# Decoder layer (state-space scan, pairwise sigmoid, mixture of experts): the stage in front of the scan reordered, the context sums taken off TensorE, high parts first, routing parts made after the second expert

## What is computed

```python
# block 1: Mamba2-like scan, 32 heads of 8, state 64, chunks of 128
xBC, z, A = split(LN(x) @ W_in.T)          # 256+2048+2048, 256, 32 columns
xBC = causal_conv4(xBC) + b; dt = softplus(A)
x = x + ((ssd_chunk_scan(...) + D * xc) * silu(z + z_bias)) @ W_out.T
# block 2: ctx is 4 x 256 x 64
si = ctx @ Wi; sj = ctx @ Wj
x = x + 0.6 * sigmoid(si[:, :, None] + sj[:, None, :] + b) + 0.4 * LN(x)
# block 3: 7 routed experts (top 2) and one shared, all of 256 x 256
u = xt @ Wup + bup; g = silu(u @ Wgate + bgate) * u
x = x + sum_e prob[e] * (g @ Wdown + bdown) + shared
```

## Time and profile before

| | |
|---|---|
| three runs | 432.19, 433.98 (median), 435.38 us |
| profiled execution, own time | 433.75 us |
| its span, first to last instruction | 432.0 us |
| mean granted TensorE clock | 0.976 |
| PE, PEld busy | 403.1, 304.4 us |
| DVE, ACT, POOL busy | 335.0, 227.7, 170.8 us |

### The profile page before, as it was taken

How to read it: one execution, slowest core, us unless ns; L and a number is a source line. 1 busy time by engine, 2 the same in 40 slices (tenths; PEclk the granted TensorE clock), 3 DMA queues, 4 the chain that set the end, 5 groups by cost and what they waited for, 6 DMA issues and landing times.

```text
span 432.0 us, 8785 instructions
## 1 busy us (share of the span) xinstructions
PE 403.1 (93%) x2989; PEld 304.4 (70%) x2989; DVE 335.0 (78%) x569; ACT 227.7 (53%) x411; POOL 170.8 (40%) x199
## 2 busy tenths in 40 slices
PE   3898999999999999999999996899999999939996
PEld 2686676676676676676666674568798888829896
DVE  4787689889898898898898838639966967826575
ACT  6766645455555455458776622474554544543631
POOL 3794110111110111105556820235675686564561
PEclk9999899999999999999999997799999999969999
DMA  7202201221012221115231140000202102000002
GB/s 213 61 1 55 57 10 56 59 59 55 15 49 56 59 57 38 29 54 132 66 100 23 47 149 2 0 0 2 74 2 73 51 24 74 0 1 2 0 1 99
DMA packets 34316, 20.54 MB, mean 48 GB/s; under 512 B 16072, under 2 KB 32144, under 8 KB 34288
## 3 DMA queue, kind: packets, MB, share of 16 engines
q1 hardware_dynamic: 34288, 20.18, 16.3%
HBM read 17.55 MB, written 1.31 MB: 44 GB/s over the span
## 4 chain that ended last, share of the span: by engine, by line
PE 79%; DVE 12%; ACT 3%; POOL 2%; issue 1%; DMA 1%; SPq 0%; DVEq 0%; ACTq 0%; POOLq 0%
PE bank L1186 28%; PE bank L1210 22%; PE bank L1413 8%; PE bank L1337 5%; PE bank L1401 4%; PE bank L1346 4%; DVE conv L963 3%; PE bank L1421 2%; PE bank L1196 2%; PE bank L1360 1%; POOL el L617 1%; DMA w_raw<-in_L_attn_W_in_dram 1%; DVE conv L1165 1%; PE bank L1381 1%; DVE utl L946 1%
## 5 line engine op out<-in xcount | busy, mean ns | idle before, releaser
L963 DVE SCALAR_TENSOR_TENSOR conv<-bank,taps,conv 128x510 f32<-128x510 f32 (+2 forms) x204 | 150.7, 745 | 25.9 <-ACT conv L650 21.1
L1210 PE MATMUL bank<-uth,parts 128*128 128x512 f32 x272 | 98.7, 413 | 2.9 <-DVE utl L946 1.6
L650 ACT ACTIVATE conv<-bank,tap_b,taps 128x512 f32<-128x512 f32 x68 | 52.9, 778 | 69.8 <-PE bank L1210 69.4
L527 POOL TENSOR_TENSOR ce<-conv,ecx 128x512 f32<-128x512 f32 x15 | 19.5, 1297 | 134.1 <-DVE conv L963 132.9
L612 POOL TENSOR_TENSOR ul<-conv,uh 128x512 fp32r<-128x512 f32 x32 | 42.7, 1349 | 48.7 <-ACT uh L865 31.0
L1210 PEld LDWEIGHTS bank<-uth,parts 128*128 128x128 f32 x272 | 51.6, 190 | 12.3 <-issue 2.2
L617 POOL TENSOR_TENSOR el<-conv,parts 128x512 fp32r<-128x512 f32 x30 | 44.0, 1489 | 34.8 <-ACT parts L877 34.7
L1210 PE MATMUL bank<-utl,parts 128*128 128x512 f32 x136 | 56.8, 418 | 0.0
L1153 DVE CAST uh<-conv 128x512 fp32r<-128x512 f32 x28 | 25.6, 949 | 28.4 <-ACT conv L861 28.1
L1048 DVE SCALAR_TENSOR_TENSOR g<-dec,bank 128x512 f32<-128x512 f32 x64 | 40.9, 679 | 1.8 <-PE bank L1337 1.7
L1413 PEld LDWEIGHTS bank<-conv 64*128 64x128 f32 x512 | 31.1, 187 | 13.9 <-DVE conv L963 7.4
(11 more groups left out here) (206 smaller groups left out, 763.2 us busy)
## 6 DMA issues: line engine op xcount, KB each, us to landing
w_raw<-in_L_attn_W_in_dram SPq DMA_DIRECT2D x17, 256.0 KB, 3.2
ecx<-ecum_dram SPq DMA_DIRECT2D x32, 128.0 KB, 2.9
ew_raw<-in_L_ffn_Wup_dram SPq DMA_DIRECT2D x7, 256.0 KB, 2.8
ew_raw<-in_L_ffn_Wgate_dram SPq DMA_DIRECT2D x7, 256.0 KB, 3.0
ew_raw<-in_L_ffn_Wdown_dram SPq DMA_DIRECT2D x7, 256.0 KB, 4.2
xres<-in_x_dram SPq DMA_DIRECT2D x2, 512.0 KB, 3.9
out_dram<-xres SPq DMA_DIRECT2D x4, 256.0 KB, 2.2
yi<-yev SPq DMA_DIRECT2D x56, 16.0 KB, 1.9
```

Of the source, the lines that this page charges most:

```text
L650: act.activation(conv[q][:, j, HALF * h:HALF * (h + 1)], bank[u % 2][:], ACT.Identity, bias=tap_b[q][:, j:j + 1], scale=taps[q][:, j, TAPS ...
L963: dve.scalar_tensor_tensor(out=dst[:, :, d:SEQ], in0=src[:, :, 0:SEQ - d], scalar=taps[q][:, j, TAPS - 1 - d:TAPS - d], in1=dst[:, :, d:SE ...
L1210: ins = pe.matmul(bank[u % 2][:], w, x_t, start=(i == 0), stop=(i == 3 * KD - 1))
```

## The change

Six parts:

1. Context sums: `si` and `sj` are now products on GpSimd (`weigh_context`, pair 1, two of 128x512) and reductions on VectorE (`sum_context`, end of pair 1). SP stores `sj` to DRAM in pair 3 and in pair 4 loads it back to every partition, one load for each sequence. TensorE's context transposes and matmuls and ScalarE's copies are gone; `halve_si` runs in pair 13.
2. The bf16 parts of the decays are made by GpSimd instead of VectorE; the table load for Exp moves from in front of the scan to the first `gate_of_z` (pair 12).
3. The order in front of the scan: project(0,0,2), (0,0,3), (1,1,0) each come one step earlier between the z tiles; W_out's transposes go to bank 7 at the end.
4. `up` and `gate` take the four matmuls of high token parts first, then the two of low parts, each with its own wait in front.
5. Between scan and experts: 9 and 3 `keep_warm` matmuls around the transposes of half 0; no `means_by_roots` where only the root is used; `shift` made later; the root for half 1 earlier on ScalarE; VectorE normalises all four tiles of half 1; gate(0) of half 0 after the transposes of half 1.
6. `prob3` is made by GpSimd after `el` of expert 1 instead of at the start of expert 6.

```diff
@@ SP
+                if n == 3:
+                    sp.wait_ge(sums_done, 2)
+                        sp.dma_start(sj_dram.rearrange("(t p) -> p t", p=P), sj[:]).then_inc(sj_out, 16)
+                if n == 4:
+                    sp.wait_ge(sj_out, 16)
+                    for b in range(NSEQ):
+                        sp.dma_start(sig[:, 2 * b, :], sj_dram[SEQ * b:SEQ * (b + 1)].partition_broadcast(P)).then_inc(sig_in, 16)
@@ GpSimd
+            pool.wait_ge(cum_done, 1)
+            link_parts(pool.tensor_copy(cparts[:, 0, :], cum[:]))
+            link_parts(pool.tensor_tensor(crest[:], cum[:], cparts[:, 0, :], ALU.subtract))
...
+            pool.tensor_copy(cparts[:, 2, :], crest[:]).then_inc(cpart_done, 1)
...
+            def weigh_context():
+                pool.wait_ge(ctx_sm_in, 32)
...
+                for i in range(2):
+                    pool.tensor_tensor(ctx_w[i], c_v, wij[:, :, CTX * i:CTX * (i + 1)].to_broadcast([P, T, CTX]),
+                                       ALU.mult).then_inc(ctx_weighed, 1)
...
+                        if isinstance(n, int) and n == 1:
+                            weigh_context()
...
-                if isinstance(e, int) and e == NE - 2:
...
+                if isinstance(e, int) and e == 1:
                     pool.wait_ge(prob_done, 1)
                     pool.tensor_copy(prob3[:, :, 2 * 32:2 * 32 + NE], prob[:])
@@ ScalarE
             def gate_of_z(v):
+                if v == 0:
+                    act.preload_act_table(ACT.Exp)
...
             normalise(T, range(2), 3)
             split_turned(4, 4)
+            split_turned(5, 5)
             root(slice(4, 8), 4)
-            split_turned(5, 5)
...
+                    if first and v == 1:
+                        root(slice(T + 4, 2 * T), 5)
                     if first and v == 2:
                         copy_logits(0)
-                        root(slice(T + 4, 2 * T), 5)
-                        normalise(T + 4, range(4, 6), 5)
@@ VectorE
-            link(dve.tensor_copy(cparts[:, 0, :], cum[:]))
...
+            def sum_context():
+                dve.wait_ge(ctx_weighed, 2)
+                for dst, v in ((si, ctx_w[0]), (sj, ctx_w[1])):
+                    dve.tensor_reduce(dst[:], v, AX.X, ALU.add).then_inc(sums_done, 1)
...
                         rest_w(n + 2, q)
+                    if u == 3 and isinstance(n, int) and n == 1:
+                        sum_context()
...
-            inverse_roots(slice(0, 4), 2, lambda: gate_last(1))
+            inverse_roots(slice(0, 4), 2, lambda: gate_last(1), False)
...
-            normalise(T + 6, range(6, 8))
+            normalise(T + 4, range(4, 8))
@@ TensorE, in front of the scan
             project_a()
             project(0, 0, 1)
             project_z(0)
+            project(0, 0, 2)
             project_z(1)
-            project(0, 0, 2)
+            project(0, 0, 3)
             project_z(2)
-            project(0, 0, 3)
+            project(1, 1, 0)
             project_z(3)
             pe.wait_ge(z_read, 2)
             turn_x(0)
             turn_x(1)
-            project(1, 1, 0)
...
+            project(1, 1, 1)
...
-            for i in range(2):
-                pe.matmul(bank[2 + i][:], wj_rep[:], ctxT[:, HALF * i:HALF * (i + 1)], start=True, stop=True).then_inc(pair_done, 1)
...
+            project(1, 1, 2)
+            turn_w(2, 1, 0, lambda: pe.wait_ge(misc_read, 1))
+            project(1, 1, 3)
             pe.wait_ge(wo_in, 16)
+            pe.wait_ge(cexp_done, 1)
@@ TensorE, after the scan
+            up_weights = ewh[0][:, 0, :, :].rearrange("p k d -> p (k d)")
+            pe.wait_ge(ewl_done, 3)
+            pe.wait_ge(o_read, 1)
+            keep_warm(2, up_weights, 9)
             turn_tokens(4, 4)
             turn_tokens(5, 5)
+            keep_warm(2, up_weights, 3)
...
+            def high_first(dst, highs, lows, before):
+                for i, (left, right) in enumerate(highs):
+                    before(i)
+                    pe.matmul(dst, left, right, start=(i == 0), stop=False)
+                for i, (left, right) in enumerate(lows):
+                    before(len(highs) + i)
+                    ins = pe.matmul(dst, left, right, start=False, stop=(i == len(lows) - 1))
...
@@ gate
-                    if m == 0:
-                        pe.wait_ge(ul_done, 4 * e + 2 * n + 2)
+                    def before(i):
+                        if m == 0 and i in (0, 2):
+                            pe.wait_ge(uh_done, 4 * e + 2 * n + i // 2 + 1)
+                        elif m == 0 and i >= 4:
+                            pe.wait_ge(ul_done, 4 * e + 2 * n + i - 3)
@@ expert 0
                     up(0, 0, range(2))
                     logits(0)
-                    gate(0, 0, range(1))
                     turn_tokens(6, 6)
                     turn_tokens(7, 7)
-                    gate(0, 0, range(1, 2))
+                    gate(0, 0, range(2))
```

More of the change, by code:

```diff
@@ L177, in decoder_layer @@
         ctx_raw = ew_raw[1][:, 0, :].rearrange("p (t d) -> p t d", t=T)
-        ctxT = ew_raw[1][0:CTX, 1:3, :].rearrange("p a n -> p (a n)")
+        ctx_w = [xn[:, 2 * i:2 * i + 2, :].rearrange("p t d -> p (t d)").rearrange("p (t d) -> p t d", t=T) for i in range(2)]
         def f32(ap):
@@ L491, in _, with copy_x @@
             pool.wait_ge(const_done, 3)
[L493 removed]
+            parts_made = [0]
+            def copy_x(m, q):
                 c0 = 2 * HD * (m - 1)
@@ L739, in pairwise @@
             def pairwise(u):
-                act.wait_ge(pair_read, 3)
+                if u == 0:
+                    halve_si()
+                    act.wait_ge(si_done, 1)
+                    act.wait_ge(sig_in, 16 * NSEQ)
                 for t in ((1, 3), (5, 7), (0, 2), (4, 6))[u]:
@@ L1086, in _ @@
             inverse_roots(slice(T, T + 4), 3)
+            shifts(range(4))
             normalise(T + 2, range(2, 4))
@@ L1299, in _ @@
             ins.then_inc(misc_turned, 1)
-            project(1, 1, 1)
             turn_x(2)
@@ L1310, in _ @@
                     c = (2 * k + j) * P
[L1311 removed]
+                    ins = pe.transpose(bank[7][:, c:c + P], wo_raw[:, j, k * P:(k + 1) * P], ident[:])
             ins.then_inc(misc_turned, 1)
[L1313 to L1325 removed]
+            pe.wait_ge(z_read, 4)
             def weigh(n, q, u):
@@ L1503, in up @@
                     at_least(pe, silu2_done, 4 * (e - 1) + v + 1)
-                    if isinstance(e, int) and e == 0 and m == 0:
-                        pe.wait_ge(utl_done, 6 + 2 * n)
-                    three(up_bank(e, v)[:], lambda k: [(ewh[q][:, 0, k, c], uth[:, k, s]), (ewh[q][:, 0, k, c], utl[:, k, s]),
-                                                 (ewl[q][:, 0, k, c], uth[:, k, s])], KD).then_inc(up_done, 1)
+                    def before(i):
+                        if isinstance(e, int) and e == 0 and m == 0:
+                            if i in (0, 2):
+                                pe.wait_ge(uth_done, 5 + 2 * n + i // 2)
+                            elif i >= 4:
+                                pe.wait_ge(utl_done, 5 + 2 * n + i - 4)
+                    high_first(up_bank(e, v)[:], [(w[q][:, 0, k, c], uth[:, k, s]) for k in range(KD) for w in (ewh, ewl)],
+                               [(ewh[q][:, 0, k, c], utl[:, k, s]) for k in range(KD)], before).then_inc(up_done, 1)
             def gate(e, q, tiles=range(4)):
```

133 lines of the change are left out of this document (58 added, 75 removed).

## The result

The changed kernel takes 420.9 us (median of four runs, 419.86 to 421.52) beside 434.13 for the kernel before: a ratio of 0.970, 95% interval 0.966 to 0.974, so 13.2 us less. The forecast was 420.0, with a range of 415.5 to 424.0. The profiled execution took 421.52, its span 419.8.

What follows compares the result with a forecast made beforehand. Bounds: TensorE waits in expert 6 and after the scan, a chain before it, TensorE's pace in the scan, the GpSimd-ScalarE-VectorE circle in experts. From 433.75, -6.5 +0.9 +0.4 +0.3 -8.6 = -13.5 gives 420.25, stated 420.0; range 415.5 to 424.0.

Steps and rivals of the forecast that it cites:

- Front, -6.5: In front of the scan: work taken off TensorE and VectorE starts the scan 6.5 us earlier, bound -4 to -7.
- The relay of projection, first tap and other taps: In front of the scan: TensorE, ScalarE and VectorE in turn set the pace; first exponents at 40.0 instead of 46.09.
- rival 2: In front of the scan: the decays' round through DRAM becomes the limit, 422 to 423 us; chance 0.10.
- Pair 1, +0.9: In the scan's pair 1: two added VectorE reductions of 0.73 us each cost 0.9 us beyond the slack (0 to 1.9).
- one slack of half a microsecond: VectorE in pair 1: half a microsecond of the 1.5 us of added reductions is absorbed, the rest counts.
- Table load, +0.4: In pair 12: the moved 1.28 us table load delays a first tap and costs 0.4 us (0 to 1.3).
- Halves, +0.3: Between scan and experts: clock held over the first hole but falling in the next, 0.3 us slower (-1.9 to +1.0).
- The 0.4 for the shorter chain to half 0: After the scan: two links of 0.2 us leave the chain to half 0, -0.4 us.
- Rival 1: Between scan and experts: the clock holds over the hole before half 1, -1.9 instead of +0.3, 418 us; chance 0.27.
- Experts, -8.6: In the experts: without the 7.4 us wait, gate(6) to the end come 8.6 us earlier, bounds -7.5 to -9.5.
- high parts first would pay for the parts: In the experts: ul may come 1.2 us later, paying for GpSimd's 0.75 us; gate(5) starts 0.5 us earlier.
- Rival 4: In the scan: SP's wait for a late store holds up load_cum(5), slower than before, 438 us at 30 us landing; chance 0.02.

Runs made afterwards that it cites:

- e8: The changed kernel with the five operations of the decays' bf16 parts back on VectorE instead of GpSimd: 420.81 us.
- e9: The changed kernel with VectorE's two context sums of pair 1 apart, one in each idle place: 419.37 us.
- e6: The changed kernel with the table load for Exp back in front of the scan: 419.73 us.
- e3: The changed kernel without its twelve warm-up matmuls: 419.81 us.
- e1: The changed kernel with the routing parts made at the start of expert 6 again: 428.85 us.
- e7: The changed kernel with up and gate in their old order of high and low parts and with their old waits: 419.94 us.
- e5: The changed kernel with GpSimd's ul of expert 0's second tile held until VectorE has normalised the four tiles of half 1: 419.32 us.
- e2: The kernel before with only the routing parts moved behind expert 1: 425.15 us.

## Why the prediction was right

- **Front, -6.5.** -6.2 were measured. The relay of projection, first tap and other taps came as walked through: exponents at 40.06 with the late DMA taken off (40.0 forecast), VectorE's idle time 1.34 us in front of the second tile of the project into bank 1 (1.35). e8 confirms how this relay absorbs work on VectorE. GpSimd's parts took 2.8 us, SP issued the load behind them at 33.9 with the late DMA taken off (33.9 forecast), and nothing waited for the decays' round through DRAM: rival 2 is out.
- **Pair 1, +0.9.** +0.74. The step was sound, the reductions are 0.6 us each and not 0.73. What the step took as one slack of half a microsecond are two (e9).
- **Table load, +0.4.** +0.48 over both periods (e6: 0.46), but in the wrong one: I forecast 14.3 us from pair 13 to 14, and it is 12 to 13 that grew, to 13.67. The load starts at 191.55, 5 us into pair 12, so what it delays is in front of the exponents of 13. No drain stands behind it: the activation starts 0.01 us after its end. By the figure in the Trainium skill (ScalarE: Activation LUTs, What ACT_TABLE_LOAD costs) the term would have been up to 1.4 larger; the measurement decides against it here.
- **Halves, +0.3.** -0.1 (and -1.0 in the second profile). Both parts of the step hold: the clock stayed up over the filled hole, with the first logits ending at 272.2 on the old scale (shifted by 3.67, the difference at pair 14; 272.4 forecast), and fell in the next hole; and four tiles on VectorE beside `ul` cost 1.06 where I had taken 1.3. The 0.4 for the shorter chain to half 0 shows as well: without warm-ups its hole is 2.20 us (e3), 2.61 before. Rival 1, the clock that holds, didn't come by itself in the changed kernel, whose ten executions have at most 0.996. Only the length at half clock was not to be foreseen: 6.8 us in one execution, 3.4 in the other.
- **Experts, -8.6.** -8.5. The parts cost 0.73 on the circle (e1), ScalarE's copies 0.54 in front of down(5) (0.7 forecast). That high parts first would pay for the parts holds up to gate(5), which comes 0.36 us earlier behind gate(0) of half 1 than before (0.5 forecast) and 1.08 earlier than in the old order (e7); of the 1.08, 0.2 are left at gate(6).
- **Rival 4,** the slower one: the store of `sj` and its four loads were issued in order, and no wait of SP for them shows. It is out.

The sum of the forecast, -13.5, met -13.6 between first matmul and end. That the two agree to 0.1 is luck: the front fell 0.3 short, the halves came 0.4 better, and in the changed kernel's other execution they came 1.3 better and the sum is -14.5. What separates 420.25 from the 421.52 profiled is the 1.36 us of the first DMA, for which no step stood.

## What to carry to other kernels

A few tenths of a microsecond of work on the wrong side of a long queue can be the most expensive lines of a kernel: look for the instruction whose input is ready long before, and whose place in its engine's order makes another engine wait. Where an engine has idle time, count its idle places one by one and give each a piece that fits, rather than adding the places up. Keep a clock warm in front of the work that has no hole behind it; in front of another hole it bought nothing here.

## Unexpected

The fall of the clock isn't tied to one hole length. The rows are the transposes of half 1 in e7 and in e5, and then those of half 0 before and in e2, whose programs are the same up to there.

```profile
272.22 1.97 PE L1280 MATMUL bank<-ident,xn 128*128 128x128 f32 x8 [3.46 <-DVE xn L977]
```

```profile
270.82 1.09 PE L1282 MATMUL bank<-ident,xn 128*128 128x128 f32 x8 [3.58 <-DVE xn L979]
```

```profile
266.66 1.94 PE L1226 MATMUL bank<-ident,xn 128*128 128x128 f32 x8 [2.61 <-ACT xn L662]
```

```profile
266.66 1.06 PE L1226 MATMUL bank<-ident,xn 128*128 128x128 f32 x8 [2.61 <-ACT xn L662]
```

In the six profiles in which the hole in front of half 1 was 4.5 to 4.7 us, the eight transposes behind it took 1.93 to 1.97 us, so it had fallen by then. Behind holes of 3.2 (e3) and 3.6 us (e5) they took 1.09, and the clock fell while TensorE was busy again, but behind one of 3.5 (e7) 1.97. Behind the same 2.61 us they took 1.94 in the one execution and 1.06 in the other. The stretch at half clock behind half 1's hole lasted between 3.4 and 6.8 us. One of the six executions of e5 (416.99 us) and one of the five of e7 (419.55) have a granted clock of 1.00 over the whole execution, so in these two it didn't fall. So a gain of a microsecond in such a stage can't be told from one execution, and a hole that fills or opens elsewhere shifts what this one costs.
